# Attention followed by a state-space scan on one Trainium2 core: drains of the gates one scan step later, and new step tables for the whole program

## What is computed

```python
# axial attention, 4 heads of 16, along j and along i
xi = _attn(x rows);  xj = _attn(x columns)      # layernorm, q/k with rotary, softmax, @Wo, elu
x  = x + (xi + xj) / 2
# state-space block on z = x
zxbcdt = layernorm(z) @ in_proj_w.T             # z_gate (128), x B C (192), dt (8)
xBC = silu(causal conv of 4 taps);  dt = softplus(dt + dt_bias)
h_t = h_(t-1) * exp(dt*A) + dt*x_t * B_t;  y_t = h_t . C_t + D * x_t     # 8 heads of 16, state 32
yg  = y * silu(z_gate)
yn  = yg * rsqrt(mean(yg**2) + eps) * ssm_norm_w;   y = yn @ out_proj_w.T
z   = z + ff(y)
out = z + fc2(gelu(fc1(layernorm(z))))
```

## Time and profile before

| | us |
|---|---|
| three timed runs | 295.57, 299.85, 300.36 (median 299.85) |
| the profiled execution | 296.06, its span 294.3 |
| PE busy in it | 229.8 (78%) |
| DVE / ACT / POOL busy | 197.8 / 164.1 / 121.0 |
| granted TensorE clock, mean | 0.942 |
| attention, up to its last step | about 0 to 122 |
| scan, first `mix` to last `mix` | 139.7 to 265.2 |
| last elementwise instruction ends | about 290.1 |

### The profile page before, as it was taken

One profiled execution on the slowest core, in us unless ns is written; L12 is line 12 of the kernel. 1 busy time (PEld: TensorE's weight loads), 2 busy tenths in 40 slices (PEclk: granted clock), 3 DMA queues, 4 the chain that ended last, 5 costly groups with the idle time before them and its releaser, 6 DMA issues. The chain is left out here.

```text
span 294.3 us, 8761 instructions
## 1 busy us (share of the span) xinstructions
PE 229.8 (78%) x3666; PEld 142.1 (48%) x3666; DVE 197.8 (67%) x333; ACT 164.1 (56%) x290; POOL 121.0 (41%) x104
## 2 busy tenths in 40 slices
PE   8956997797888986669698799849977777955383
PEld 3634665565656753627463376325432434434141
DVE  2799578678887862667888655694169595385513
ACT  2256774876777688275548921931583528723340
POOL 1825797635537004028621753148658341300000
PEclk9998799999999999999999799995998979999859
DMA  6932222111211002104000610000000000011003
GB/s 176 343 42 88 74 77 90 38 38 41 73 38 38 4 2 70 41 0 107 2 0 3 166 45 2 1 3 2 2 0 2 0 2 1 2 35 39 1 0 71
DMA packets 25223, 12.96 MB, mean 44 GB/s; under 512 B 22240, under 2 KB 22496, under 8 KB 25056
## 3 DMA queue, kind: packets, MB, share of 16 engines
q1 hardware_dynamic: 23456, 11.24, 13.5%
q10 hardware_dynamic: 1728, 1.17, 1.5%
HBM read 4.63 MB, written 1.05 MB: 19 GB/s over the span
## 5 line engine op out<-in xcount | busy, mean ns | idle before, releaser
L1673 POOL TENSOR_TENSOR a_msk<-dt_fin,c_sb 128x512 f32<-128x512 f32 x32 | 38.7, 1208 | 31.2 <-issue 13.5
L1257 DVE TENSOR_TENSOR mix<-dec,g_m 128x512 f32<-128x512 f32 x32 | 30.0, 944 | 5.2 <-ACT dec L1515 4.6
L1659 POOL TENSOR_TENSOR dtx<-xv,dt_fin 64x512 f32<-64x512 f32 x16 | 20.2, 1265 | 27.2 <-PE p_turn L603 9.5
L603 PEld LDWEIGHTS p_turn<-mix,dtx 128*32 128x32 f32 x512 | 11.7, 116 | 35.6 <-DVE mix L1257 23.0
L603 PE MATMUL score<-a_msk,c_sb 128*128 128x512 f32 x44 | 26.0, 674 | 1.5 <-POOL a_msk L1673 1.5
L1426 ACT ACTIVATE prob_t<-p_turn 128x512 f32<-128x512 f32 x32 | 17.4, 594 | 14.8 <-PE p_turn L608 14.6
L603 PE MATMUL p_turn<-mix,dtx 128*32 128x64 f32 x512 | 18.7, 237 | 8.6 <-DVE mix L1257 8.5
L1168 DVE TENSOR_REDUCE s_max<-score 128x16 f32<-128x1024 f32 x16 | 19.5, 1217 | 5.5 <-PE score L603 5.4
L954 ACT ACTIVATE sqr<-cen 128x512 f32<-128x512 f32 (+1 forms) x13 | 7.7, 593 | 26.5 <-DVE cen L947 26.5
L1515 ACT ACTIVATE dec<-score 128x512 f32<-128x512 f32 x22 | 13.0, 589 | 13.7 <-PE score L603 13.7
L1437 ACT ACTIVATE prob<-s_cen 128x1024 f32<-128x1024 f32 x16 | 16.9, 1054 | 6.5 <-DVE s_cen L1180 6.3
(11 more groups left out here) (185 smaller groups left out, 551.0 us busy)
## 6 DMA issues: line engine op xcount, KB each, us to landing
rot_swap<-rot_sin SPq DMA_DIRECT2D x28, 128.0 KB, 2.1
p_sb<-params SPq DMA_DIRECT2D x1, 1520.0 KB, 9.8
x_tok<-x SPq DMA_DIRECT2D x16, 64.0 KB, 3.9
ut_a<-u SPq DMA_DIRECT2D x8, 126.0 KB, 2.7
ut_b<-u SPq DMA_DIRECT2D x8, 124.0 KB, 2.7
ut_b<-u SPq DMA_DIRECT2D x8, 122.0 KB, 2.4
out<-x_tok SPq DMA_DIRECT2D x10, 64.0 KB, 2.2
back<-x ACTq DMA_DIRECT2D x4, 128.0 KB, 5.7
```

What stands on the lines that cost most here:

```text
L603: return pe.matmul(dst, lhsT, rhs, start=start, stop=stop, skip_group_check=True)
L1257: v.tensor_tensor(mix[:, e % LAPS, :, :], dec[:, e % LAPS, :, :], wide(g_m[:, e // 4 % 2, e % 4, :], SSM_H), ALU.mult)\
L1659: gp.tensor_tensor(dtx[rows, k % 2, :, :, s, :].rearrange("p t h n -> p (t h) n"), xv[rows, 4 * k:4 * k + 4, :].rearrange("p t (h n) -> p ...
L1673: gp.tensor_tensor(a_msk[:, m % LAPS, :, :], deep(dt_fin[:, 0, SSM_H * m:SSM_H * (m + 1)], GRID), wide(cst("tri"), SSM_H), ALU.mult).then_ ...
```

## The change

The engines' instructions stay what they are, and so does their number; where they stand in the lists changes.

1. **Gates.** DVE forms `z_s` of a gate half in the step after the one in which PE makes the product and ACT the tanh, right behind `mix` and `y_g` and ahead of the step's other uses. Before, it was in the same step.
2. **Tables of their own** for the mean (`MEAN_STEP`), the projection (`PROJ_STEP`) and the turn (`JOIN_STEP`); before, mean and projection shared `PROJ_STEP` and the turn was one step later.
3. **All tables set anew.** The attention's q, k, v uses are now a written list `ATT_AT` of (kind, group, 3*step + slot). Those that move:

| use | step and slot before | after |
|---|---|---|
| attention: bo | 3c | 4a |
| attention: wo 0 (and its elu) | 5a | 6a |
| attention: v 3 | 6b | 6a |
| attention: q 5, k 6, q 6 | 7c, 8c, 9c | 7b, 8b, 9b |

| use in the scan | step m before | after |
|---|---|---|
| xt 2, 3 | 0, 1 | 1, 2 |
| xp 4 to 7 | 2 2 3 3 | 3 3 3 3 |
| xp 8 to 15 | 8 8 9 9 10 10 11 11 | 8 9 10 10 10 11 11 12 |
| x_tanh 2 | 3 | 2 |
| bc 2 | 11 | 10 |
| gate halves z0, z1 of chunks 0 to 3 (PE and ACT) | 1,2; 6,7; 11,12; 20,21 | 1,3; 6,6; 11,11; 19,21 |
| the same on DVE | 1,2; 6,7; 11,12; 20,21 | 2,4; 7,7; 12,12; 20,22 |
| squares of groups 3, 4 | 31, 33 | 30, 32 |
| turn `yo` of group 3 | 33 | 34 |
| ht and layernorm of groups 0, 1 | 25, 27 | 24, 28 |
| f2, fo of group 1 | 30, 31 | 31, 33 |
| f2 of group 2 | 38 | 39 |

The mean and the projection keep the same steps: `MEAN_STEP` and `PROJ_STEP` hold equal numbers.

```diff
--- before.py
+++ after.py
@@ -69,35 +69,19 @@
 
 
 
-WO_STEP = (5, 7, 9, 11, 13, 15, 17)
-XT_STEP = (14, 17, ATT_STEPS, ATT_STEPS + 1)
-UT_STEP = (16, BETWEEN, ATT_STEPS + 6, ATT_STEPS + 7)
-XP_STEP = (18,) * 4 + tuple(ATT_STEPS + m for m in (2, 2, 3, 3, 8, 8, 9, 9, 10, 10, 11, 11))
-NORM1_STEP = (15, 18, ATT_STEPS + 5, ATT_STEPS + 5)
+WO_STEP = (6, 7, 9, 11, 13, 15, 17)
+XT_STEP = (14, 17, 20, 21)
+UT_STEP = (16, -2, 25, 26)
+XP_STEP = (18, 18, 18, 18, 22, 22, 22, 22, 27, 28, 29, 29, 29, 30, 30, 31)
+NORM1_STEP = (15, 18, 24, 24)
+ATT_AT = (('xr', 1, 0), ('k', 1, 0), ('q', 1, 0), ('xr', 2, 4), ('k', 2, 5), ('q', 2, 7), ('v', 1, 10), ('xr', 3, 8), ('k', 3, 11), ('bo', 0, 12), ('q', 3, 13), ('k', 4, 14), ('v', 2, 16), ('q', 4, 17), ('v', 3, 18), ('k', 5, 20), ('q', 5, 22), ('v', 4, 25), ('q', 6, 28), ('k', 6, 25), ('v', 5, 31), ('k', 7, 32), ('q', 7, 35), ('v', 6, 37), ('v', 7, 43))
 
 
 def attention_uses():
 
     steps = {-1: ([("xr", 0), ("k", 0), ("q", 0), ("v", 0)], [], [])}
     for n in range(ATT_STEPS):
-        g, odd = divmod(n, 2)
-        if n == 0:
-            a, b, c = [("xr", 1), ("k", 1), ("q", 1)], [], []
-        elif n == 1:
-            a, b, c = [], [("xr", 2)], [("k", 2)]
-        elif n == 2:
-            a, b, c = [], [("q", 2)], [("xr", 3)]
-        elif n == 3:
-            a, b, c = [], [("v", 1)], [("k", 3), ("bo", 0)]
-        elif n == 4:
-            a, b, c = [], [("q", 3)], [("k", 4)]
-        elif n == 5:
-            a, b, c = [], [("v", 2)], [("q", 4)]
-        elif odd:
-            a, b, c = [], [], [("q", g + 2)]
-        else:
-            a, b, c = [], [("v", g)], [("k", g + 2)]
-        a, b, c = ([(kind, k) for kind, k in uses if 0 <= k < ATT_CHUNKS] for uses in (a, b, c))
+        a, b, c = ([(kind, k) for kind, k, at in ATT_AT if at == 3 * n + slot] for slot in range(3))
         if n == FOLD_STEP:
             c.append(("fold", 0))
         (a if n < 17 else c).extend(("wo", k) for k, at in enumerate(WO_STEP) if at == n)
@@ -113,10 +97,12 @@
 
 
 GROUPS = ((0, 8), (8, 16), (16, 24), (24, 28), (28, 32))
-SQUARE_STEP = (20, 22, 27, 31, 33)
+SQUARE_STEP = (20, 22, 27, 30, 32)
+MEAN_STEP = (22, 24, 29, 32, 34)
 PROJ_STEP = (22, 24, 29, 32, 34)
-NORM_STEP = (25, 27, 32, 35, 37)
-MLP_STEPS = ((28, 29, 30), (28, 30, 31), (37, 38, 39), (38, 39, 40), (38, 39, 40))
+JOIN_STEP = (23, 25, 30, 34, 35)
+NORM_STEP = (24, 28, 32, 35, 37)
+MLP_STEPS = ((28, 29, 30), (28, 31, 33), (37, 39, 39), (38, 39, 40), (38, 39, 40))
 TAIL_STEP = 33
 SSM_STEPS = 41
 LAPS = 3
@@ -124,11 +110,11 @@
 
 
 DT_PARTS = ((0, CT), (CT, 2 * CT), (2 * CT, TILES))
-LOG_STEP = (ATT_STEPS + 4, ATT_STEPS + 12)
-DT_STEP = ((18, 18, 18), (ATT_STEPS + 4, ATT_STEPS + 5, ATT_STEPS + 5), (ATT_STEPS + 12, ATT_STEPS + 13, ATT_STEPS + 13))
-BC_STEP = (None, 3, 11, 20)
-Z_STEP = ((1, 2), (6, 7), (11, 12), (20, 21))
-X_TANH_STEP = {3: 2, 4: 3, 9: 4, 10: 5, 11: 6, 12: 7}
+LOG_STEP = (23, 31)
+DT_STEP = ((18, 18, 18), (23, 24, 24), (31, 32, 32))
+BC_STEP = (None, 3, 10, 20)
+Z_STEP = ((1, 3), (6, 6), (11, 11), (19, 21))
+X_TANH_STEP = {2: 2, 4: 3, 9: 4, 10: 5, 11: 6, 12: 7}
 X_SILU_STEP = {4: 2, 6: 3, 10: 4, 11: 5, 12: 6, 13: 7}
 
 
@@ -146,8 +132,9 @@
         steps[Z_STEP[c][0]].append(("z0", c))
         steps[Z_STEP[c][1]].append(("z1", c))
     for o in range(len(GROUPS)):
-        steps[PROJ_STEP[o]] += [("ms", o), ("op", o)]
-        steps[PROJ_STEP[o] + 1].append(("yo", o))
+        steps[MEAN_STEP[o]].append(("ms", o))
+        steps[PROJ_STEP[o]].append(("op", o))
+        steps[JOIN_STEP[o]].append(("yo", o))
     for o in range(len(GROUPS)):
         steps[NORM_STEP[o]].append(("ht", o))
     for o in range(len(GROUPS)):
@@ -1265,11 +1252,13 @@
                     half = 4 * (k % 2)
                     v.tensor_tensor(y_g[:, c, :, half:half + 4, :], YT[k % 2][:, :].rearrange("p (t h j) -> p h t j", t=4, h=2),
                                     z_s[:, c % 2, :, half:half + 4, :], ALU.mult).then_inc(gated, 1)
+                if m >= 1:
+                    for use in ssm_steps[m - 1]:
+                        if use[0] in ("z0", "z1"):
+                            z_use(use)
                 for use in ssm_steps[m]:
                     kind, c = use
-                    if kind in ("z0", "z1"):
-                        z_use(use)
-                    elif kind in ("xt", "xp"):
+                    if kind in ("xt", "xp"):
                         att_use(use)
                     elif kind == "op":
                         w = in_chunk(c)
```

## The result

| | us |
|---|---|
| changed kernel, four timed runs | 279.6, 280.2, 281.03, 281.56 (median 280.62) |
| kernel before beside it, four runs | 293.81, 295.57, 299.85, 300.36 (median 297.71) |
| ratio, with its 95% interval | 0.950 (0.943 to 0.957) |
| profiled execution, its span | 280.2, 278.4 (before 296.06, 294.3) |
| mean granted clock in it | 0.959 (before 0.942) |

A forecast was written before the change was run, and what follows sets the result against it. No engine full over the span; PE bound from 200 to 216, elsewhere engines waiting in turn. Terms of 16.3 less 3.5 give 12.8, so 283.3 from 296.06; plus 1.9 for the median, 285.0, range 277 to 295.

The forecast's parts named there:

- Attention: Attention: q 5, k 6, q 6 ahead of the V product and wo 0 out of step 5 save 1.2 us.
- Opening: Scan steps 0 to 5: later xt 2 and the gate's wait of 1.42 gone save 1.4 us.
- Steps 6 to 13: Gates of chunks 1 and 2: shorter waits and softplus right behind xp 15 save 3.5 us.
- POOL's wait under 5: Sign of being right: POOL's wait for dt_fin, 8.29 us before, falls under 5.
- Steps 19 to 22: Gate half 0 of chunk 3 goes ahead of B and C, removing DVE's 6.60 wait: 2.9 us saved.
- Steps 23 to 29: Group 0's layernorm finished in step 23 and its transposes a step earlier save 3.7 us.
- Steps 30 to 34: Output steps: f2 and fo of group 1 later, squares earlier, yo 3 later save 2.4 and 1.2 us.
- The end: f2 of group 2 behind f1 of groups 3 and 4: gain 0, last sum within 0.5 us of before.
- Take-back: `mix` meets more of POOL's work in a shorter scan, which takes back 3.5 us of the gain.
- the clock: Rival, chance 0.09: shorter waits keep PE's clock at 2.4 GHz, more comes off, 281.5 us.
- held bank: Rival, chance 0.08: PE stands for each gate's bank, freed a step later by DVE; slower, 309 us.
- waits under another name: Rival, chance 0.21: ACT's list is the new bound, half the terms of steps 0 to 29 stay, 291 us.

The follow-up runs named there:

- the first pair of executions: Profiled executions of the kernel before (296.06 us) and of the changed kernel as first run (280.2 us).
- the second: The changed kernel run again with nothing altered, set against the kernel before: median 279.4 us, ratio 0.948.
- the late drain alone: The kernel before with one edit, DVE multiplying a gate a step behind its products, all tables old: 293.8 us, ratio 0.995 to the kernel before.
- the tables alone: The changed kernel with DVE multiplying a gate in the step of its products again, all tables new: 286.9 us, ratio 0.971 to the kernel before.

## Why the prediction was right

The range and the direction held, and 280.6 lies 4.4 under the 285.0. Of that, 3.1 is the sum (283.3 for an execution like the profiled one, which took 280.2), the rest comes from the 1.9 that I added for the median: here the median is only 0.4 over the profiled execution. That the sum came so near is in part luck; by its own steps:

- **Attention**: 1.2 in the first pair of executions, 2.2 over fourteen. Unit 6 came 3 sooner and unit 7 did not, as worked out.
- **Opening**: this step failed. It gave -1.2 in the first pair and +0.15 in the second, for +1.4; with the clock alike, about nothing. What I took "at nothing", x_tanh 2, is worth nothing; ACT does stand there, over the 3 that I had given as a sign against me, and it costs nothing. What I left out was that the late drain holds a bank here (3.09 with the old tables), and that PE has most of these 20 us full. I had counted waits of DVE and ACT in front of PE's products without asking when PE would have made them.
- **Steps 6 to 13**: 3.6 for 3.5, but before had 3.4 us at half clock in it and the changed kernel none, so the order's part is 1.9 to 2.6. The cause was shared wrongly, too: I gave most of it to the order of softplus and xp. From `mix` 4 to 7 the late drain alone takes 8.02, both 8.43, the tables alone 10.63, all at full clock, so it is the drain's; from `mix` 7 to 15, where softplus and xp are, both take 29.7 for 30.3. The sign "POOL's wait under 5" was missed: it is 6.33 for 8.29.
- **Steps 19 to 22**: 3.9 for 2.9 up to the projection of group 0. The wait of 6.60 went to 1.28; with the gate behind B and C again, 2.2 come back. `op` 0 waits 2.08 for PE, where I had no wait. The excess is the clock: low from 194 to 198 only, where before it was low from 198 to 206. With 6.8 us at half in all, from `mix` 15 to `op` 0, it is 24.99 before and 22.66 in two executions of the new order: 2.3.
- **Steps 23 to 29**: 3.3 for 3.7, and here too a step failed. With the clock alike it is 1.6, and undoing the tables that it was forecast for gives none of it back. DVE's wait of 3.33 is 0.50, but the layernorm ahead of it now takes its time from the same list, 0.70 and 1.05 of waits included; the projection of group 1 comes 10.02 behind that of group 0, undone 9.74.
- **Steps 30 to 34**: 2.5 and 1.3 for 2.4 and 1.2, with the clock at 1.00 in both; the waits named went, and undone they came back. This is the part that was right by its mechanism and its size.
- **The end**: 1.0 for 0. Up to DVE's first f2 it is 6.03 behind the last xhat for 6.15 before, so the order gave 0.1, near the 0 forecast; the other 0.9 comes behind it (3.81 for 4.70), where the granted clock is 1.00, and before was 0.50 up to 287. All three executions with the old end are low there, so order and clock can't be told apart in it.
- **Take-back, 3.5**: mis-sized. `mix` has a mean of 994 ns for 944, so 32 x 0.05 = 1.6, and DVE's busy time in all fell from 197.8 to 194.8. The rule of the Trainium skill (SBUF — State Buffer, "Who interferes with whom") agrees with single rows (1.54 beside POOL again, 0.68 alone), but a shorter span met little more of it. (The ends that I gave for it are 0 and 8.1, not 8.3: 0.944 - 0.69 is 0.254.)

```profile
L1244 DVE TENSOR_TENSOR mix<-dec,g_m 128x512 f32<-128x512 f32 x32 | 31.6, 994 | 2.3 <-ACT dec L1504 1.6
```

With the clock alike, then, as far as single executions tell, the stages add up to 2.2 + 0 + 2.3 + 2.3 + 1.6 + 3.8 + 0.1 = 12.3, near the forecast 12.8, but it is terms 4 us smaller than forecast and not the 3.5 taken back that bring it there. The rest of the measured gain goes with the clock: the changed kernel's nine runs have a mean of 0.948, the 42 of the kernel before beside the experiments 0.924, and among those 42 a clock higher by 0.01 goes with 1.2 us less, which makes 2 to 3 us. That was the rival of 0.09, "the clock"; whether the orders raised the clock or chance did, no run shows.

Of the signs named: no wait over 1 us before gates is nearly so (1.30 and 1.28 stand); projection of group 0 came 7.8 sooner for 9, that of group 2 11.1 for 12; from `mix` 20 on gaps over 4 us remain (7.6 from `mix` 22 to 23, for 4.5 before), which I had said would not. Idle time on PE ended by L1225, the sign of the held bank, is 2.2. The held bank, at 0.08, was a real mechanism (7.4 us of PE's waiting with the old tables), hidden by the new tables. The waits under another name did come, in part: of the 11.5 forecast for steps 0 to 29 about 6.2 are there with the clock alike, a little over the half that this rival kept.
